# Cross-attention with key latents as the stationary operand, probabilities scaled before their transposition, and quantisation scalars on GpSimd

## The reference

```python
q_c = q @ W_dq;  kv_c = kv @ W_kvc                       # 96 and 64 latents
scores = (q_nope . k_nope + rope(q_rope) . rope(k_rope)) * scale   # 16 heads
scores = where((k_ids <= seg) & (k_ids >= seg - 8), scores, -1e30)
attn = softmax(scores)
x = x + tanh(g0) * (einsum('bhqk,bkhd->bqhd', attn, v).reshape(...) @ W_o)

def bitlinear158(x, w, b):            # act_quant: scale = 127 / max(|x|, 1e-5)
    return act_quant(rms_norm(x)) @ weight_quant(w).T + b
h = layer_norm(gelu(silu(bitlinear158(layernorm(x), w1, b1))))     # 1024 wide
x = x + tanh(g1) * bitlinear158(h, w2, b2)
```

## Time and profile before

| | us |
|---|---|
| median of 3 runs | 273.82 (273.74 to 274.13) |
| span of the profiled execution | 272.2 |
| set-up until the first scores | 49 |
| tiles 1 to 6, each | 23.5 to 24.0 |
| tail behind tile 7 | 34.3 |

### The profile page before, as it was taken

The page is one execution under the profiler, slowest core; times in us unless marked ns, Lnnn a source line. Parts: engine busy times, 40 slices in busy tenths (PEclk is TensorE's granted clock), DMA queues, the critical chain, the costliest instruction groups (busy, mean ns, idle before and its releaser), DMA issues.

```text
span 272.2 us, 5124 instructions
## 1 busy us (share of the span) xinstructions
PE 234.8 (86%) x1653; PEld 206.2 (76%) x1660; DVE 204.5 (75%) x510; ACT 147.8 (54%) x329; POOL 85.4 (31%) x126
## 2 busy tenths in 40 slices
PE   1899999998999999799899999989999986935354
PEld 1676688987989899799899889989988976722233
DVE  2595304366896765999999899999989997889871
ACT  2366220562455663745775494677549558859131
POOL 1335402242361322354233444423343440102210
PEclk9999655699999999999999999999999999995557
DMA  6999990000000000000000000000000000000000
GB/s 196 291 185 230 349 365 4 4 0 0 2 2 0 0 2 2 2 0 4 0 20 0 0 0 19 0 0 19 0 0 0 19 2 0 22 0 0 20 19 28
DMA packets 11349, 12.31 MB, mean 45 GB/s; under 512 B 3936, under 2 KB 10336, under 8 KB 11104
## 3 DMA queue, kind: packets, MB, share of 16 engines
q1 hardware_dynamic: 10432, 11.44, 15.3%
q10 hardware_dynamic: 896, 0.61, 0.7%
HBM read 11.00 MB, written 1.05 MB: 44 GB/s over the span
## 4 chain that ended last, share of the span: by engine, by line
PE 39%; DVE 34%; issue 14%; POOL 6%; ACT 3%; DVEq 2%; DMA 1%; POOLq 0%; SPq 0%
PE bank_pair L778 5%; DVE qcat L1120 4%; PE bank_ff L904 4%; POOL h_small L433 3%; PE bank_lat L885 3%; DVE h L1210 3%; PE bank_score L862 3%; DVE turned L1124 3%; DVE z L1189 3%; DVE neg_max L1269 3%; PE bank_ff L933 2%; PE bank_swap L781 2%; DVE h L1179 2%; DVE lat L1280 2%; PE bank_prob L874 2%
## 5 line engine op out<-in xcount | busy, mean ns | idle before, releaser
L407 POOL TENSOR_TENSOR qcat<-qcat,turned 64x256 f32<-64x256 f32 x32 | 23.0, 720 | 113.4 <-DVE turned L1124 113.4
L631 ACT ACTIVATE prob_room<-bank_score,neg_max 128x128 f32<-128x128 f32 x128 | 36.5, 370 | 20.2 <-DVE neg_max L1269 19.8
L778 PE MATMUL bank_pair<-qcT,wcat 96*128 96x128 f32 (+1 forms) x256 | 36.7, 290 | 0.0
L862 PEld LDWEIGHTS bank_score<-kcat,qcat 128*128 128x128 f32 x256 | 34.5, 196 | 2.3
L885 PE MATMUL bank_lat<-kvc,probT_room 128*128 128x65 f32 (+1 forms) x256 | 32.7, 271 | 3.5 <-ACT probT_room L621 3.5
L1120 DVE TENSOR_TENSOR qcat<-bank_pair,cst 128x512 f32<-128x512 f32 x32 | 21.9, 683 | 17.8 <-PE bank_swap L781 17.8
L885 PEld LDWEIGHTS bank_lat<-kvc,probT_room 128*128 128x128 f32 x256 | 31.1, 192 | 4.9 <-ACT probT_room L621 4.9
L862 PE MATMUL bank_score<-kcat,qcat 128*128 128x128 f32 (+1 forms) x256 | 34.6, 280 | 0.0
L778 PEld LDWEIGHTS bank_pair<-qcT,wcat 96*128 96x128 f32 x256 | 33.6, 205 | 0.5 <-issue 0.4
L409 POOL TENSOR_TENSOR qcat<-qcat,turned 64x256 f32<-64x256 f32 x32 | 30.5, 953 | 2.5
L612 ACT COPY latT<-bank_lat 128x256 f32<-128x256 f32 x32 | 11.8, 369 | 34.6 <-PE bank_lat L892 34.6
(11 more groups left out here) (165 smaller groups left out, 441.4 us busy)
## 6 DMA issues: line engine op xcount, KB each, us to landing
wo<-in_L_xattn_W_o SPq DMA_DIRECT2D x1, 2048.0 KB, 19.7
w_sb<-in_L_ffn_w SPq DMA_DIRECT2D x2, 1024.0 KB, 10.5
out_x<-y SPq DMA_DIRECT2D x8, 128.0 KB, 1.7
wuq<-in_L_xattn_W_uq SPq DMA_DIRECT2D x1, 768.0 KB, 10.9
ctx_all<-in_ctx ACTq DMA_DIRECT2D x2, 256.0 KB, 4.8
x_all<-in_x SPq DMA_DIRECT2D x2, 256.0 KB, 4.6
cst<-in_consts SPq DMA_DIRECT2D x1, 512.0 KB, 6.8
x_all<-in_x SPq DMA_DIRECT2D x1, 512.0 KB, 7.7
```

What stands on the lines that cost most here:

```text
L407: nc.gpsimd.tensor_tensor(odd, odd, add_odd, ALU.add).then_inc(pair_half, 1)
L631: last = nc.scalar.activation(prob[:, k % 2, j, 0:kts * P], src[:, j, :], ACT.Exp, bias=neg_max[:, k % 2, j:j + 1])
L778: nc.tensor.matmul(bank_pair[:, (2 * j + e) * P:(2 * j + e + 1) * P], wcat[:, 2 * k + j, e, :], src, start=True, stop=True)
L862: last = nc.tensor.matmul(bank[:, j * kts * P:(j + 1) * kts * P], qcat[:, k, hh // 2, hh % 2, :], kcat[:, b, hh % 2, 0:kts * P], start=Fal ...
```

## The change

1. Value product. kvc1 loses its column of ones and becomes the stationary operand (64 columns); the transposed probabilities move, two heads at a time. The even heads go to output partitions 0 to 63, the odd ones to 64 to 127. The result is already the transposed latents, so transpose_lat, the tile lat and two semaphores go.
2. The row sum comes from the exponentials (accum_out to esum).
3. normalise scales the probabilities (128x512, in place) by the reciprocal of esum, and does it before they are transposed; it now stands ahead of turn_step on VectorE, and transpose_probs waits for it.
4. Quantisation. GpSimd computes x's mean square, a floor and the factor for dequantisation; VectorE's quantise has three operations in place of five, residual_and_quantise loses two more.
5. The loops over tiles are written out as straight code, and so is the loop of stores.
6. At the end ScalarE copies the last latents ahead of silu.

```diff
@@ gpsimd
+            def floor_and_root(small_of, floor_ready):
+                link(small(small_of(FLOOR), small_of(MS), pos_half, ALU.pow))
+                nc.gpsimd.tensor_scalar(small_of(FLOOR), small_of(FLOOR), 1e-5 / QMAX, 1.0, ALU.mult, ALU.mult).then_inc(floor_ready, 1)
+                link(small(small_of(RRMS), small_of(MS), neg_half, ALU.pow))
             def root_hq(c):
                 pool.wait_ge(h_sumsq, c + 1)
                 link(small(hs(MS), hs(SQ), eps1, ALU.add))
-                small(hs(RRMS), hs(MS), pow_half, ALU.pow).then_inc(h_rrms, 1)
+                floor_and_root(hs, h_floor)
             def root_x(c):
                 pool.wait_ge(x_moments, c + 1)
-                small(xs(RRMS), xs(MS), pow_half, ALU.pow).then_inc(x_root, 1)
+                link(nc.gpsimd.tensor_scalar(xs(VAR), x_mv[:, 1:2], EPS, EPS, ALU.add, ALU.mult))
+                link(small(xs(MS), xs(VAR), x_mv[:, 1:2], ALU.add))
+                floor_and_root(xs, x_floor)
+            def dequantise(small_of, layer, deq, scale_ready, count, deq_ready):
+                pool.wait_ge(scale_ready, count)
+                nc.gpsimd.tensor_scalar(deq, small_of(YMAX), small_of(RRMS), wmean[:, layer:layer + 1],
+                                        ALU.mult, ALU.mult).then_inc(deq_ready, 1)
@@ scalar, exponentials
+                if n >= 2:
+                    act.wait_ge(rsum_done, n - 1)
                 for j in range(GROUP):
                     last = nc.scalar.activation(prob[:, k % 2, j, 0:kts * P], src[:, j, :], ACT.Exp,
-                                                bias=neg_max[:, k % 2, j:j + 1])
+                                                bias=neg_max[:, k % 2, j:j + 1], accum_out=esum[:, k % 2, j:j + 1])
@@ tensor
             def transpose_probs(f, k, kts):
                 n = step_no(f, k)
-                pe.wait_ge(exp_done, n + 1)
+                pe.wait_ge(prob_scaled, n + 1)
...
             def values(f, k, kts):
-                for j in range(GROUP):
-                    for kt in range(kts):
-                        last = nc.tensor.matmul(bank_lat[:, j * (KVC + 1):(j + 1) * (KVC + 1)], probT[:, k % 2, kt, j, :],
-                                                kvc1[:, b * KT + kt, :], start=(kt == 0), stop=(kt == kts - 1))
+                for kt in range(kts):
+                    for o in range(2):
+                        last = nc.tensor.matmul(bank_lat[o * KVC:(o + 1) * KVC, 0:2 * P].rearrange("p (j s) -> p j s", j=2),
+                                                kvc1[:, b * KT + kt, :], probT[:, k % 2, kt, o::2, :],
+                                                start=(kt == 0), stop=(kt == kts - 1))
...
-                        if not known(f) or 2 <= n < N + 2:
-                            transpose_lat(*behind(f, k, 2))
@@ vector
-            def quantise(src, small, layer, amax, root, count, deq, ready):
-                dve.wait_ge(root, count)
-                dve.wait_ge(dve_link, links["base"] + amax)
-                link(nc.vector.tensor_scalar(small(YMAX), small(AMAX), small(RRMS), 1e-5, ALU.mult, ALU.max))
-                nc.vector.tensor_scalar(deq, small(YMAX), 1.0 / QMAX, wmean[:, layer:layer + 1], ALU.mult, ALU.mult)
-                link(nc.vector.reciprocal(small(YINV), small(YMAX)))
-                link(nc.vector.tensor_scalar(small(QMUL), small(YINV), QMAX, small(RRMS), ALU.mult, ALU.mult))
+            def quantise(src, small, amax, floor, scale, count, ready):
+                dve.wait_ge(floor, count)
+                dve.wait_ge(dve_link, amax)
+                nc.vector.tensor_scalar(small(YMAX), small(AMAX), 1.0 / QMAX, small(FLOOR), ALU.mult, ALU.max).then_inc(scale, 1)
+                dve.wait_ge(scale, count)
+                link(nc.vector.reciprocal(small(QMUL), small(YMAX)))
                 nc.vector.tensor_scalar(src, src, small(QMUL), MAGIC, ALU.mult, ALU.add).then_inc(ready, 1)
...
+            def normalise(f, k, kts):
                 n = step_no(f, k)
+                dve.wait_ge(exp_done, n + 1)
+                nc.vector.reciprocal(rsum[:, k % 2, :], esum[:, k % 2, :]).then_inc(rsum_done, 1)
                 dve.wait_ge(rsum_done, n + 1)
+                p = prob[:, k % 2, :, 0:kts * P]
+                nc.vector.tensor_tensor(p, p, rsum[:, k % 2, :].unsqueeze(2).broadcast_to([P, GROUP, kts * P]),
+                                        ALU.mult).then_inc(prob_scaled, 1)
...
                         softmax_max(f, k, kts)
+                        if n >= 1:
+                            normalise(*behind(f, k, 1), kts)
                         if n + AHEAD < N:
                             turn_step(*ahead(f, k))
-                        if not known(f) or 1 <= n < N + 1:
-                            normalise(*behind(f, k, 1))
```

More of the change, by code:

```diff
@@ L109, in build @@
         half_neg = sb("half_neg", [P, F])
+        half = sb("half", [P, 1])
         eps = sb("eps", [P, F])
@@ L286, in choose, with run_tiles @@
                 main(KT)
-        LEAD = 3
-        def run_tiles(eng, body, after, before=lambda f: None):
-            for f in range(LEAD):
-                before(f)
+        def run_tiles(body, after):
+            for f in range(F):
                 body(f)
-            before(None)
-            with eng.Fori(LEAD, F - 1) as f:
-                before(f)
-                body(f)
-            before(F - 1)
-            body(F - 1)
             after()
         def slot(c):
-            return 1 if known(c) and c == F - 2 else 0
+            return 1 if c == F - 2 else 0
         def last_tile(c):
-            return known(c) and c == F - 1
+            return c == F - 1
         def down_bank(c):
@@ L315, in there @@
         def there(f, lag):
-            return not known(f) or 0 <= f - lag < F
+            return 0 <= f - lag < F
         def score_banks(k, kts):
@@ L375, in _ @@
             out_v = out.rearrange("b (t p) d -> (b t) p d", p=P)
-            with sp.Fori(0, F) as f:
+            for f in range(F):
                 sp.wait_ge(y_done, f + 1)
-                sp.dma_start(out_v[bass.ds(f, 1), :, :].rearrange("o p d -> p (o d)"), y[:, :]).then_inc(out_stored, 16)
+                sp.dma_start(out_v[f, :, :], y[:, :]).then_inc(out_stored, 16)
             sp.wait_ge(out_stored, 16 * F)
@@ L382, in _ @@
         def _(pool):
-            half = R // 2
+            rope = R // 2
             pool.wait_ge(consts_made, 1)
@@ L410, in add_rope @@
                 pool.wait_ge(pair_done, s + 1)
-            with pool.Fori(0, B // 2) as i:
-                for e in range(2):
-                    b = 2 * i + e
-                    add_rope(kcat[KVC:P, b, 0, :], kcat[0:R, b, 1, :], turned[KVC:P, e, :], turned[0:R, e, :], b)
+            for b in range(B):
+                add_rope(kcat[KVC:P, b, 0, :], kcat[0:R, b, 1, :], turned[KVC:P, b % 2, :], turned[0:R, b % 2, :], b)
             def add_rope_step(f, k):
@@ L607, in copy_latT @@
             def copy_latT(f, k):
-                n = step_no(f, k)
-                act.wait_ge(latT_ready, n + 1)
-                if not (known(f) and f == 0):
+                act.wait_ge(lat_ready, step_no(f, k) + 1)
+                if f > 0:
                     act.wait_ge(attn_ready, f)
@@ L616, in copy_probT @@
                 n = step_no(f, k)
-                if not (known(n) and n < 2):
+                if n >= 2:
                     act.wait_ge(lat_ready, n - 1)
@@ L811, in prepare_end @@
             def prepare_end(f, k):
-                if known(f) and f == 0:
+                if f == 0:
                     if k == 1:
@@ L849, in scores @@
                 lag = 1 if kts == 1 else 0
-                if not (known(n) and n <= lag):
+                if n > lag:
                     pe.wait_ge(exp_done, n - lag)
@@ L918, in up @@
                 pe.wait_ge(xqT_copied, c + 1)
-                if waits and not (known(c) and c < 2):
+                if waits and c >= 2:
                     pe.wait_ge(y_done, c - 1)
@@ L1137, in prepare @@
             def prepare(f, k):
-                if not known(f):
-                    return
                 if f == 0 and k in (1, 2):
@@ L1241, in output @@
                                                     ALU.mult, ALU.add))
-                if not (known(c) and c == 0):
+                if c > 0:
                     dve.wait_ge(out_stored, 16 * c)
@@ L1327, in after @@
                     output(F - 1)
-                run_tiles(dve, body, after, before)
+                run_tiles(body, after)
             choose(dve, main)
```

167 lines of the change are left out of this document (71 added, 96 removed).

## The result

The changed kernel takes 374.79 us (median of four runs, 372.59 to 376.98) where the kernel before takes 273.92 (273.74 to 274.13): a ratio of 1.368, interval 1.3607 to 1.3752. The profiled execution took 372.83 us, of which 369.2 are the span: 97.0 us more span than before. Medians and ratios are of fast runs alone: one run, of the changed kernel with the old scalars, was in a slower state and is left out.

What follows compares the result with a forecast made beforehand. VectorE's program was taken to set the steady pace, TensorE to end last in the first three tiles. Span 272.2 + 69.2 for the change + 9.5 for the clock = 350.9; with 1.6 outside, 352 us, range 336 to 376.

Steps and rivals of the forecast that it cites:

- The ring: Each step, maximum (start M), scaling, transpositions, projection, turning in series: feed-forward at M + 4.61, +2.46 us where VectorE sets the pace.
- The terms inside it: Step prices in the steady part, such as four records of values at 0.47 us against 0.84 for today's eight.
- The warm k = 3: Last step of a steady tile at full clock: 7.4 us between maxima.
- The clock: TensorE's granted clock halves after long idle stretches in tiles 3 to 7: +9.5 us, bounds 0 and +30.
- one fall in each of five tiles: Of two 4.3 us idle stretches per tile, one is followed by half clock, costing 1.9 us more.
- the hand-over: VectorE to TensorE to VectorE in each step, with no other work to fill it: +2.46 us where VectorE set the pace.
- the upper bound: Both idle stretches of a tile bring half clock, with more lost in the output product: +30 us.
- The clock stays low through the steady part: Rival: 1.9 us more in each of 20 steps, output product 3.5 us longer; +50, 393 us; chance 0.07.
- The early tiles: Steps 1 to 11 (tiles 0 to 2), where VectorE's present waits absorb some of the cost: +20.1 us.
- The end: From step 30, accumulator reads and later exponentials: +4.1 us at the last residual; three quantisations in the tail: -0.8.
- The scalars: In k = 2, 0.65 us taken off VectorE is returned by GpSimd's longer chain: zero.
- The straight code: Loops written out save issue time in four passes: -0.8 us; fetching the longer program: 0 to +2.

Runs made afterwards that it cites:

- the old scalars: Changed kernel with the quantisation scalars as before (VectorE does the small operations, GpSimd only the root): 371.3 us, ratio 1.3553.
- the order of the waits alone: Kernel before with one wait added: transpositions of the probabilities of step n-1 also wait for the maximum of step n; 362.53 us, ratio 1.3273.
- distance: Changed kernel with transpositions of probabilities, their copies and values of step n-2, not n-1, done in step n: 283.15 us, ratio 1.0308.
- the turned order: Changed kernel with projection ahead of transpositions on TensorE and turning ahead of scaling on VectorE: 386.72 us; with the scaling also moved to GpSimd, 306.02 us.
- the scaling at the head of GpSimd's step: Changed kernel with transpositions, copies and values one step later, probabilities scaled first in GpSimd's step, and quantisation scalars as before: 282.96 us, ratio 1.0303.

## Why the prediction was right, and where it was off

*The ring* was right in place and size: M + 3.59 and M + 4.53 against M + 3.67 and M + 4.61; the order of the waits alone gives 89 of 101 us, and removing it by distance takes 92 away (both with the clock's part in them). In tiles 3 to 6, with the clock all but held up, the kernel has 39.5 us more than before (134.3 against 94.8) where the sum without its clock term had 40.4.

*The terms inside it* erred both ways and nearly cancel. Four records of values take 0.58 to the next start (324.32 to 324.90), not 0.47; still 0.26 under today's 0.84. The warm k = 3 was 6.9 us, not 7.4.

*The clock* is the term that was mis-sized. Span with and without it differ by 21.1 us (369.2 and 348.1), where I took 9.5 with bounds 0 and 30. The step that failed: "one fall in each of five tiles", 1.9 each, for the hand-over alone. There were two falls in each tile: both long idle stretches of the tile of 184 to 223 (3.82 and 4.18 us) were followed by half clock, and in each of tiles 3 to 6 the steps k = 1 and k = 3 are 1.2 to 3.7 us longer than with the unused matmuls (k = 1: 11.6, 12.9, 12.2 and 10.5 against 9.3; k = 3: 9.6, 8.3, 8.4 and 9.3 against 6.9). Falls came in tiles 0 to 2 as well, where I had none. A fall cost the hand-over 1.7 us (M + 5.25 against M + 3.59), a little less than my 1.9, but the low clock lasted into the output product, 5.57 us instead of 3.7, which ended behind VectorE's work and left VectorE idle for 1.90 ahead of the next maximum (row 205.77). Two falls in a tile and the slow output product were in my text, as the upper bound and in the rival "The clock stays low through the steady part", but not in the sum; falls in tiles 0 to 2 were nowhere. That the total still lay inside the range is owed to its width: the range ended at 376, the median is 374.79, and two of the four runs lie above 376. Row 243.57 of the earlier trace rows had shown a fall behind 3.73 us idle; with 4.3 us forecast at two places of each tile, two falls were what that row spoke for.

*The early tiles* were 28.5 us longer, not 20.1. With the clock up they still are 23.7 longer, so at least 4.8 is the clock and at most 3.6 the hand-over, of which the waits of the first tiles hid less than I had taken (in tile 1 the clock still fell there, to 0.84).

*The end* was 6.5 longer, not 3.3. All of it lies ahead of the last addition to x: that comes 15.8 us behind the last maximum (336.92), before 9.3 (239.88), 6.5 more where I had 4.1; behind it nothing changed (32.3 us both times), where I had -0.8. The accumulator reads are not the reason, as they were dearer in my sum (1.9 us for four) than on the chip (1.5). But TensorE has one more fall of the clock there, which the sum did not have. It idles 3.20 us until the last probabilities are scaled, and the window behind that, from 329.00 to 333.00, is at 0.57; before, the window from 231.00 to 240.00 had 1.00:

```profile
329.37 1.11 PE L877 MATMUL bank_prob<-cst,prob_room 128*128 128x128 f32 x4 [3.20 <-DVE prob_room L1268]
330.70 1.49 PE L921 MATMUL bank_ff<-w1T,xqT 128*128 128x512 bf16 x3 [0.22 <-issue]
...
329.00:333.00 4.00, 3.37 (x11) 1.58 (x12) 1.02 (x3) 0.58 (x1) 0.91 (x2) 0.57 0.00 0
```

The kernel with the unused matmuls idles the same 3.20 us there, its clock falls too (0.52 from 309.50 to 313.00), and its end is 6.6 longer. How much of the missing 3.2 us that fall explains was not measured. The straight kernel's profiled execution also has an end 1.2 us longer than before (42.8 against 41.6), so the straight code may have a part in it.

*The scalars* on GpSimd cost about 3 us, not zero: the chain starts behind the rope additions and VectorE waits 0.88 us for it.

*The straight code* was forecast at 0.8 us less. In the span it gives 1.8, but outside the span most straight kernels have 3 to 4 us where the kernel before has 1.6 to 1.9. In the profiled execution of the result it is 3.6, 2.0 over my forecast, and the median lies another 2.0 above that execution.

In sum: forecast span 350.9, measured 369.2; of the 18.3 between them the clock is 11.6, the early tiles at full clock 3.6, the end 3.2, and what is left, both ways, about zero.

## What to carry to other kernels

Before moving an operation ahead of another engine's, write down for both engines what stands behind the new wait; if the wait and its release lie in the same step, the step can become a ring. Here another order only moved it, and a step more of distance cut it. Price a new idle stretch on TensorE twice, once as idle time and once as the work at half clock behind it; and price it at every place where it recurs, the tail too. And when an engine's work is taken away, ask first whether that engine is ever waited for: here TensorE lost 192 instructions and the kernel was no faster than before even with the ring gone.

## What the runs showed of the hardware

*Work for nothing can pay.* Filling two idle stretches of a tile with unused matmuls raised the granted clock of the window from 140 to 200 us from 0.78 to 1.00 and made the kernel 22 us faster.

*Less work on VectorE went with a lower clock on TensorE.* The kernel with the scaling at the head of GpSimd's step has 2.8 us less of VectorE's work in a tile; in three of its four middle tiles TensorE's granted clock fell to between 0.90 and 0.93, and they were 1.6 to 2.4 us longer than the one at 1.00.

*VectorE and GpSimd slow one another.* In the kernel with the turned order the scaling (two inputs in SBUF) runs beside GpSimd's rope additions:

```profile
225.44 0.71 POOL L397 TENSOR_TENSOR qcat<-qcat,turned 64x256 f32<-64x256 f32 x1 [4.19 <-DVE turned L1118]
225.47 1.23 DVE L1268 TENSOR_TENSOR prob_room<-prob_room,rsum 128x512 f32<-128x512 f32 x1
226.23 1.06 POOL L399 TENSOR_TENSOR qcat<-qcat,turned 64x256 f32<-64x256 f32 x1
```

The multiplication takes 1.23 us instead of 0.69, and the second addition 1.06 instead of 0.72 (the least of this group). The one that began first kept its length: the addition ends at 226.15, and about 0.55 us later the multiplication is over; the second addition ends some 0.6 after that. The Trainium skill ("SBUF — State Buffer", Who interferes with whom) says that a VectorE instruction with two inputs in SBUF contends with a GpSimd instruction that reads SBUF, that the pair of ports they share is an exclusive lock, and that the order of issue decides which of the two is blocked. The order of these rows agrees with that; both that came second end 0.1 us earlier than if they had been held up for the whole length of the first.

*The time outside the span is not a constant of the chip.* It was 1.6 us in the profiled execution of the kernel before (1.8 to 1.9 in its later runs), 3.1 to 4.0 for the same kernel in straight code and 3.2 to 3.7 for the change, but 1.8 to 1.9 for the change with the unused matmuls, which is straight code too. What sets it stays open.
